# An attention and expert kernel on one core: GpSimd makes the low half of every fourth weight piece

## What is computed

```python
def _L0_xattn_ref(q, k, v, igate_w, igate_b, fgate_w, fgate_b, out_w):
    gi = jnp.concatenate([q, k, v], axis=-1)
    ig = (gi @ igate_w.T + igate_b).transpose(0, 2, 1)
    fg = (gi @ fgate_w.T + fgate_b).transpose(0, 2, 1)
...
    cs = jnp.cumsum(jax.nn.log_sigmoid(fg), axis=-1)
    log_D = jnp.where(mask, cs[..., :, None] - cs[..., None, :], -jnp.inf) + ig[..., None, :]
    max_log_D = jnp.max(log_D, axis=-1, keepdims=True)
    C = qk * jnp.exp(log_D - max_log_D)
    normalizer = jnp.maximum(jnp.abs(C.sum(-1, keepdims=True)), jnp.exp(-max_log_D))
    h = jnp.einsum('bhst,bhtd->bhsd', C / (normalizer + EPS), vh)
...
def _L0_ffn_ref(x, gate_w, w1, b1, w2, b2):
    gate_scores = jax.nn.softmax(xf @ gate_w, axis=-1)
    topk_scores, topk_idx = jax.lax.top_k(gate_scores, TOP_K)
    h = jax.nn.gelu(jnp.einsum('td,edf->etf', xf, w1) + b1[:, None, :], approximate=False)
    y = jnp.einsum('etf,efd->etd', h, w2) + b2[:, None, :]
...
x = x + _L0_xattn_ref(_layernorm(x, axis=-1), ctx_1024, ctx_1024, ...)
x = x + _L0_ffn_ref(_layernorm(x, axis=-1), ...)
```

## Time and profile before

| | us |
|---|---|
| median of 3 runs | 671.48 |
| lowest and highest | 670.55, 677.57 |
| span of the profiled execution, first to last instruction | 672.2 |
| its own time as a run | not given |
| DVE busy in the span | 489.8 (73%) |
| PE busy in the span | 626.9 (93%) |
| ACT busy in the span | 323.3 (48%) |
| POOL busy in the span | 187.1 (28%) |

### The profile page before, as it was taken

One profiled execution on the slowest core, in us unless ns is written; L12 is line 12 of the kernel. 1 busy time (PEld: TensorE's weight loads), 2 busy tenths in 40 slices (PEclk: granted clock), 3 DMA queues, 4 the chain that ended last, 5 costly groups with the idle time before them and its releaser, 6 DMA issues. The chain is left out here.

```text
span 672.2 us, 20373 instructions
## 1 busy us (share of the span) xinstructions
PE 626.9 (93%) x6736; PEld 533.2 (79%) x6737; DVE 489.8 (73%) x1330; ACT 323.3 (48%) x767; POOL 187.1 (28%) x185
## 2 busy tenths in 40 slices
PE   1799998999889899999999999999999999999985
PEld 1567876778677668988989898988889898988774
DVE  2457988979889898985889866757675757666562
ACT  2668888777878746543332232323232323232321
POOL 3000003231323315135345332313141323233112
PEclk9899999969999999999999999999999999999998
DMA  4534537654644636333374423233232323133100
GB/s 139 156 106 148 160 94 231 188 189 144 207 152 137 199 103 208 77 70 78 66 221 93 68 40 61 43 56 46 46 52 44 57 39 64 35 65 53 21 4 1
DMA packets 55036, 66.55 MB, mean 99 GB/s; under 512 B 5472, under 2 KB 50720, under 8 KB 54832
## 3 DMA queue, kind: packets, MB, share of 16 engines
q1 hardware_dynamic: 41552, 48.13, 24.1%
q0 software_dynamic: 13296, 17.32, 14.1%
q10 hardware_dynamic: 112, 0.08, 0.1%
HBM read 41.50 MB, written 24.92 MB: 99 GB/s over the span
## 5 line engine op out<-in xcount | busy, mean ns | idle before, releaser
L1038 ACT ACTIVATE decay_slots<-scores,b_turned 128x256 f32<-128x256 f32 (+1 forms) x312 | 124.4, 451 | 257.4 <-PE scores L1519 244.9
L1519 PE MATMUL scores<-x_slots,w_halves 128*128 128x256 f16 (+1 forms) x1872 | 203.3, 264 | 0.8 <-issue 0.8
L1519 PEld LDWEIGHTS scores<-x_slots,w_halves 128*128 x1872 | 173.4, 98 | 23.3 <-issue 1.4
L641 POOL DMA_INDIRECT expert_rows<-xf_rows,slot_i x64 | 66.7, 1042 | 224.1 <-issue 114.8
L1533 PE MATMUL pv<-w_halves,decay_slots 128*128 x864 | 97.7, 273 | 0.0
L663 POOL DMA_INDIRECT out_rows<-v_centred_and_one,row_ids x36 | 57.8, 1605 | 138.8 <-DVE v_centred_and_one L2111 96.1
L1533 PE MATMUL gate_bank<-w_halves,q_and_k_halves 128*128 x840 | 95.0, 273 | 0.0
L1533 PEld LDWEIGHTS pv<-w_halves,decay_slots 128*128 128x128 f16 x864 | 84.1, 98 | 10.5 <-issue 0.3
L1533 PEld LDWEIGHTS gate_bank<-w_halves,q_and_k_halves 128*128 128x128 f16 x840 | 81.8, 98 | 10.1
L663 POOL DMA_INDIRECT out_rows<-work,row_ids x35 | 55.3, 1580 | 112.1 <-DVE work L2111 84.7
L1257 PEld LDWEIGHTS pv<-v_centred_and_one,decay_slots 128*128 128x128 f32 x512 | 64.5, 197 | 1.6
(11 more groups left out here) (257 smaller groups left out, 845.5 us busy)
## 6 DMA issues: line engine op xcount, KB each, us to landing
weight_stage<-in_L_ffn_w SPq DMA_DIRECT2D x32, 512.0 KB
x_slots<-in_x SPq DMA_DIRECT2D x16, 512.0 KB
weight_stage<-expert_rows SPq DMA_DIRECT2D x30, 272.0 KB
ctx_slots<-in_ctx SPq DMA_DIRECT2D x8, 512.0 KB
out_rows<-x_slots SPq DMA_DIRECT2D x8, 512.0 KB
v_centred_and_one<-expert_rows SPq DMA_DIRECT2D x9, 272.0 KB
expert_rows<-v_centred_and_one SPq DMA_DIRECT2D x9, 272.0 KB
expert_rows<-xf_rows,slot_i POOLq DMA_INDIRECT x64
```

Of the source, the lines that this page charges most:

```text
L641: pool.indirect_dma_start(table, bass.IndirectOffsetOnAxis(ap=sloti[:, step[1], j, k:k + 1], axis=0), xfn[:, step[1], j, :], None, bounds_ ...
L1038: ins = act.activation(hf[:, f * R:f * R + tr.rows(0)], ps_s[:, q, n * R:n * R + tr.rows(0)], ACT.Gelu, bias=b1T[:, bass.ds(expert, 1), f] ...
L1519: ins = pe.matmul(o, w, xh[:, tr.slot(0) % 2, b, k, 0:tr.rows(0)], start=(n == 0), stop=(n == 3 * KC - 1))
```

## The change

Piece 3 of every step (the second half of an expert's w2) gets its low half from GpSimd. [...] GpSimd's order is: pieces of steps 0, 1 and 2, the scatter of step 0, and in each loop turn first the piece of `nxt`, then the scatter of `last`. VectorE's eight calls `weights_low(..., 3)` go. `s_lo` counts three pieces for each step instead of four, and SyncE's load of piece 1 waits for `s_lp`, the others for `s_lo`. SyncE before the first rows of tiles and TensorE before the feed-forward part wait for the last `s_lp`.

```diff
--- before.py
+++ after.py
@@ -264,6 +264,8 @@
         s_w = [sem(f"weights_in{p}") for p in range(2)]
         s_hi = sem("weights_high")
         s_lo = sem("weights_low")
+        s_lp = sem("weights_low_by_pool")
+        s_ls64 = sem("weights_scaled_by_pool")
         c_dn = Chain(sem("dve_next"), DVE_NEXT)
         c_dh = Chain(sem("dve_here"), DVE_HERE)
         c_an = Chain(sem("act_next"), ACT_NEXT)
@@ -424,8 +426,11 @@
                 def weights(step, n):
 
                     g, half, q = number(step), n % 2, n // 2
-                    if n >= 2 or some(step, 1):
-                        sp.wait_ge(s_lo, g * 4 + (n - 1))
+                    if n != 1 and (n or some(step, 1)):
+                        sp.wait_ge(s_lo, g * 3 + max(n - 1, 0))
+                        sp.sem_inc(s_held, 1)
+                    elif n == 1 and some(step, 1):
+                        sp.wait_ge(s_lp, g)
                         sp.sem_inc(s_held, 1)
                     dst = stage[:, half, :]
                     if half:
@@ -540,7 +545,8 @@
                 for p in range(2):
                     for done in s_sc[p]:
                         sp.wait_ge(done, SLOTS_FULL[p] * SCATTERED)
-                sp.wait_ge(s_lo, 4 * NSTEP)
+                sp.wait_ge(s_lo, 3 * NSTEP)
+                sp.wait_ge(s_lp, NSTEP)
                 for k in range(3):
                     load(Turn(0, 0), k)
                 sp.wait_ge(s_pv, (NSTEP - 1) * SB)
@@ -643,11 +649,27 @@
                                 xfn[:, step[1], j, :], None, bounds_check=TABLE - 1,
                                 oob_is_err=False).then_inc(s_sc[step[1]][k], 16)
 
+                def weights_low(step):
+
+                    g = number(step)
+                    pool.wait_ge(s_hi, g * 4 + 4)
+                    pool.sem_inc(s_held, 1)
+                    hi, lo = (w2s[:, bass.ds(g, 1), a, FC // 2:FC, :].rearrange("p a c d -> p (a c d)")
+                              for a in range(2))
+                    pool.tensor_scalar(stage[:, 1, :], stage[:, 1, :], W_SCALE, None, ALU.mult).then_inc(s_ls64, 1)
+                    pool.wait_ge(s_ls64, g + 1)
+                    pool.tensor_tensor(lo, stage[:, 1, :], hi, ALU.subtract).then_inc(s_lp, 1)
+
                 def body(last, step, nxt, after):
+                    if nxt is not None:
+                        weights_low(nxt)
                     if last is not None:
                         scatter(last)
 
                 def first_steps():
+                    weights_low(S0)
+                    weights_low(S1)
+                    weights_low(S2)
                     scatter(S0)
 
                 first_steps()
@@ -1565,6 +1587,7 @@
                             routing()
 
                 pe.sem_inc(s_l2, L20)
+                pe.wait_ge(s_lp, NSTEP)
                 sixth, last = NEXT_LAST, LAST
                 scores(last, 3)
                 stream_before(last, 2, 3)
@@ -1916,7 +1939,6 @@
                         x1_of(step)
                     if nxt is not None:
                         c_of(nxt, 1)
-                        weights_low(nxt, 3)
                     if nxt is not None and after is None:
                         early_counts()
                         early_list()
@@ -1943,7 +1965,6 @@
                     max_log_decay(S0)
                     c_of(S0, 0)
                     next_stats(S2)
-                    weights_low(S0, 3)
                     c_of(S0, 1)
                     gate_bias(S1)
                     weights_low(S1, 0)
@@ -1963,7 +1984,6 @@
                     c_of(S1, 0)
                     x1_of(S0)
                     gate_bias(S2)
-                    weights_low(S1, 3)
                     x1_stats(S0)
                     c_of(S1, 1)
                     x1_norm(S0)
@@ -1988,7 +2008,6 @@
                     gate_bias(S3)
                     x1_stats(S1)
                     c_of(S2, 1)
-                    weights_low(S2, 3)
                     log_f(S3)
                     records(S0)
 
```

## The result

| | before | after | ratio, 95% interval |
|---|---|---|---|
| first series | 671.98 us (4 runs, 670.55 to 677.57) | 679.14 us (4 runs, 677.94 to 682.43) | 1.0098 [1.0050, 1.0147] |
| a later series | 671.93 us (35 runs, 668.18 to 679.87) | 677.26 us (12 runs, 668.48 to 680.92) | 1.0037 [0.9998, 1.0075] |

The changed kernel is slower by 5 to 7 us at the median, where 2 us less was forecast. Ratios leave disturbed executions out, but that does not explain why the second ratio is nearer to 1 than its medians: without those executions the medians are 677.09 and 671.70 us, 1.0080. The interval of the second ratio just holds 1, so only the first series is clear of noise by its ratio. The profiled execution after took 679.28 us, with a span of 677.2 us (a run's time is some 2 us above its span).

What follows compares the result with a forecast made beforehand. Before the feed-forward part the wait that ends last bounds, TensorE standing higher than VectorE (busy 0.87); -3.4 - 0.5 + 0.3 + 1.6 = -2.0 us gives a median of 669.5 us, range 665.5 to 676.0.

Steps and rivals of the forecast that it cites:

- Steps 0, 1 and 2: I take 0: First three steps: VectorE's removed pieces give TensorE no gain, taken as 0.
- Two engines on one memory: GpSimd's pair beside VectorE's work: 0.4 us in each of four turns, +1.6 us; high end 2.4 us a turn.
- Rival 1: VectorE stands behind GpSimd at sum L1757 and small operations before the second product: +7, 678.5 us; chance 0.14.
- Rival 5: TensorE's clock: 666.5 us if the low stretch of 133 to 163 us goes, 672.5 if another comes; chance 0.13.
- The scale: GpSimd's scale of 128x1024, sized from a select and an iota: 1.3 us.
- the subtraction: GpSimd's two-input subtraction of 128x1024: 2.4 us taken; 2.25 by the skill's halved figure.
- The pair: GpSimd's scale and subtraction with the wait between: 3.8 us taken, ends 2.4 and 6.9.
- rival 4: GpSimd's pair takes 6.9 us; first turn pays 3.6, second about 1: +2.3, 673.8 us; chance 0.08.
- The context, +0.3: First loop turn: context load slips 1.4 us behind GpSimd, +0.3 us taken, ends -1.1 and +3.6; later turns no cost.
- The gain in the loop, -3.4 - 0.5: TensorE's shorter waits: up to 3.4 us before the turnings of steps 3 to 5, 0.5 in step 6.
- rival 2: Nothing comes through: the guess follows TensorE, three turns give 0.4 instead of 1.14; +0.2, 671.7 us; chance 0.20.
- The feed-forward part: After the attention steps: no instruction changes; it starts 2 us earlier and keeps its length.

Runs made afterwards that it cites:

- run 4: Kernel before, VectorE making all pieces, with an idle GpSimd scale and subtraction beside it in steps 0 to 5: 688.06 us, ratio 1.0181.
- run 5: Changed kernel plus seven filler matmuls in TensorE's idle time of step 1: 673.35 us, ratio 1.0011.
- run 14: Changed kernel, but VectorE makes piece 3 in step 1; no fillers, SyncE's order as it was: 674.11 us, ratio 1.0004.
- run 11: Changed kernel measured again without any edit: 677.26 us, ratio 1.0037.
- run 9: Changed kernel with GpSimd making piece 3 in steps 3 to 7 only, and SyncE issuing the context load first: 670.86 us, ratio 0.9964.
- run 12: Changed kernel with both the seven fillers in step 1 and the context load first: 668.61 us, ratio 0.9941.
- run 15: Changed kernel with VectorE making piece 3 in step 1, and the context load first, no fillers: 670.70 us, ratio 0.9942.
- run 1: Changed kernel with GpSimd making piece 3 in steps 3 to 7 only, VectorE in steps 0 to 2: 674.99 us, ratio 1.0019.
- run 7: Changed kernel with the context load ahead of weight piece 1 and the x1 write, GpSimd's pair whole: 672.73 us, ratio 0.9991.
- run 10: Kernel before with the context load first on SyncE and nothing else: 671.31 us, ratio 0.9978.

## Why the prediction was wrong, point by point

- **What failed first: "Steps 0, 1 and 2: I take 0".** That was right for the gain and said nothing of a loss. The loss is in step 1: 1.3 us of TensorE's idle time behind a VectorE instruction that GpSimd holds, and 4.7 us that the work at 1.2 GHz behind it takes longer. (A second part lies in the loop, behind the context; see below.) The traces of runs 4, 5 and 14 against after and 11 show this chain. How much it costs in a typical execution is less sure: by their ratios only runs 9, 12 and 15, all with the context first, lie clear of run 11.
- **"Two engines on one memory": 1.6 us from a scatter beside the statistics.** The nearest row was of another kind: that scatter did not hold VectorE, and the statistics are not held even by the subtraction (1.39 us at 161.48, inside the subtraction of 161.06). In the profiled execution VectorE is held at seven of the eight pairs, by 0.4 to 1.5 us at the start of the scale or by up to 2.0 us behind the subtraction; in step 1 nothing absorbs it. In the loop one turn shows it in full, where a gate operation (0.19 us elsewhere) is held and TensorE waits for the product behind it; step 6's first product loses 1.55 us by it:

```profile
217.09 1.73 DVE L1658 SCALAR_TENSOR_TENSOR minus_abs_f<-gates 128x32 f32<-128x32 f32 x1
220.01 0.51 PE L1222 MATMUL scores<-q_and_k_halves 32*128 32x128 f16 x24 [1.13 <-DVE decay_slots L1737]
```

The sum took 0.4 us in each of four turns, 1.6, and none in the first steps; step 1 alone cost 6.0 us with the clock. The right bound was the other one in the same passage, the whole subtraction. The Trainium skill (SBUF — State Buffer, Who interferes with whom) says it as an exclusive lock; for the subtraction the trace agrees (2.03 us, and the piece of 2.31 us in run 4), and where VectorE's two-operand x1 sum was first, GpSimd stood instead (2.59 us at 132.56 for the usual 2.13).
- **Rival 1 had the mechanism and nearly the time** (678.5), in the wrong place. It looked at the x1 sum and priced the loop; the decisive spot was `var_eps_x` of step 1. The 1.03 us of waiting that were to absorb most of it belong to one turn of the kernel before, behind its short slow stretch at 182 to 186 us; at the same place of after VectorE waits 0.15 us (192.73).
- **Rival 5 named the clock and kept it apart from rival 1.** In step 1 they are one chain: the stall makes idle time, and the low clock follows it. Priced together, rival 1 would have had step 1 at 6 us.
- **The scale was mis-sized:** 1.3 us taken, 2.84 measured. For the subtraction 2.4 was taken; it measured 2.25 in the mean and 2.13 where nothing holds it. The Trainium skill's figure (GPSIMD Engine Reference, 3.1 Elementwise), halved to 2.25, agrees with that within 6%. The pair is 5.1 us, not 3.8, between the forecast and rival 4.
- **The context, +0.3.** The forecast had the load late in the first turn and "earlier, no cost" in the later ones. It was the other way: from the issue of the context to the fourth product, behind which it is needed, the first four turns have 5.9, 7.2, 7.7 and 7.6 us before, and 7.0, 6.4, 6.0 and 6.5 after. The turn that the forecast took as its example was one in which VectorE's second product was late. In after TensorE waited once, 2.6 us, in the third turn, with 10 us at 1.2 GHz behind it; run 1 had 2.4 us in the first turn with no pair before it. Runs 7 and 12 against 11 and 5 put the share of SyncE's order at 0.5 to 0.7%. By itself the order gives 0.2% on the kernel before, not told from nothing (run 10). For the flight I took 6.4 us without a row of its own; in after it was 5.9 to 8.5 from 65 us on.
- **The gain in the loop, -3.4 - 0.5, was right at VectorE:** 1.1 us in each of steps 3 to 6, 4.5 in all, and the fourth products keep it. VectorE's wait for ScalarE's guess stays 0.42 us (169.73), so the guess moves with VectorE, and rival 2 is out. In after only 1.3 us came through to the end of the loop: the held instructions and the wait for the context took the rest. That run 9's profiled execution wins 4.1 us is in part its clock.
- **The feed-forward part** kept its length: from the last product to the end 421.1 us before, 420.2 after.

What stays open: how the loss divides between lock and queue in a typical execution. The two remedies give 0.3 to 0.9% (fillers or step 1 left out) and 0.5 to 1.1% (order), against 1.0037 and 1.0098 for the changed kernel, and their intervals overlap. Which of TensorE's waits in the loop is followed by a slow stretch differs between executions, and it was not tried to hold the clock through all of them.

## What to carry to other kernels

Work moved to an idle GpSimd is not free for VectorE: look at every VectorE instruction that can fall beside GpSimd's two-operand operation, the tiny ones too, and ask who waits for it. Price an idle time of TensorE together with the slow work that follows it, and read the number of matmuls in a stretch beside the busy time. When a load's release moves to another engine, list what is queued behind it; putting the load with the least room first is a cheap remedy, and with the two remedies the changed kernel runs 0.6% below the kernel before. The kernel before with the same two edits is 0.1% below itself, so about 0.45% is what the change is worth by these runs, with intervals that just overlap.

## What was not expected of the hardware

- GpSimd's TENSOR_SCALAR over 128x1024 float32 has records of 2.77 to 3.14 us, longer than its TENSOR_TENSOR (2.12) with two inputs. But VectorE is held only for its first part: `minus_abs_f` at 43.96 stands until 44.59, 1.1 us after the scale began, and VectorE's piece, two SBUF operands, runs its usual 1.23 us from 45.25 beside the rest of it, which is recorded to 46.29. A lock held for the whole record does not fit that. The Trainium skill (Perfetto Trace Analysis, GPSIMD Engine Instruction) calls a GpSimd instruction's span in a profile unreliable; these rows agree. So does the gate operation at 217.09: it takes 0.19 us elsewhere, and is held before the record of the scale begins at 217.69.
- Cut to a quarter, the scale takes 0.955 us and the subtraction 0.698: 0.22 us of a subtraction and 0.35 of a scale are fixed (estimates from four quarters against a whole one of 2.12 and 2.77 us), and a pair in quarters costs 6.6 us for 5.1.
- Executions of one kernel differ by 10 us and more, and the difference goes along with the mean clock: among the 35 runs of before, 668.18 us at 0.988 and 678.08 at 0.972. A change's median is in part a statement on how often TensorE falls to 1.2 GHz.
